# GpSimd makes all ten low halves of the held-back expert weights in the token stage

## The chip, the cores and the metric

The program runs on one core of one Trainium2 chip, in one launch. What is measured is the device time of that launch in microseconds (us). PE is the matrix engine (TensorE), DVE the vector engine, ACT the scalar engine, POOL is GpSimd, and SP is the engine that issues most of the DMAs.

## The reference

The computation is one transformer layer on 8 sequences of 256 tokens of width 512 (2048 tokens): cross-attention, then a mixture-of-experts feed-forward block with two routed experts per token and one shared expert.

```
x = x + attention(layernorm(x), ctx) @ Wfc.T + bfc      # 32 query heads, 8 key/value groups, head width 16
h = layernorm(x)
w = two_best(softmax(h @ gate_weight.T))                # 8 experts in 4 groups, best 2 groups, best 2 experts
g, u = h @ gate_w[n].T, h @ up_w[n].T                   # n = 0..7, inner width 352; the shared expert has 704
routed = sum_n w[n] * ((silu(g) * u) @ down_w[n].T)
x = x + routed + (silu(h @ sh_gate.T) * (h @ sh_up.T)) @ sh_down.T
```

## The kernel before

All matrix products of the feed-forward block are made in float16 with a correction: each float32 weight is scaled by a power of two and cut into a **high half** (the scaled value rounded to float16) and a **low half** (what the rounding left, again in float16). PE then runs three products for one: high by high, high by low, low by high.

The gate and up weights are ten matrices (eight experts and the shared one in two parts), each handled as two pieces of 128 partitions by 1408 columns, so there are 20 pieces (`CUTS`). Ten are cut during attention. The other ten (`2 * HELD`, those of experts 0 to 4) are held back, since attention's own buffers lie where they go, and are cut in the **token stage**, the stage this text is about.

The token stage goes over 16 tiles of 128 tokens. For each tile t, in program order on each engine:

- PE: transposes the normalised tile t-2 (line 1439), transposes the attention output of tile t+1 (line 1422), multiplies tile t by Wfc (line 1430, 8 matmuls), and makes the gate logits of tile t-3 (line 1448).
- ACT: copies the transposed tile t-2 out twice (lines 1065 and 1066), copies the transposed attention output of tile t+1 out (line 1060, `ot_evac`), makes a square root (line 1074), copies logits (line 1070), then makes the high half of piece h = t-2 (line 1100, `first_part`), then normalises tile t (line 1079). PE's line 1430 of a tile cannot start before ACT's line 1060 for that tile.
- DVE: residual sum (line 1931), statistics (lines 1933 to 1935), low half of the transposed tile t-2 (line 1917), the reciprocal square root (lines 1689 to 1697), and the shift of the normalisation (line 1940). After every odd tile up to 11 it makes the low half of one held-back piece (line 1965), for h = 1, 3, 5, 7, 9.
- GpSimd: makes the low halves for h = 0, 2, 4, 6, 8. [...]
- SP issues the loads and stores of the tiles.

The raw pieces come by DMA (704 KB each) into a **ring of three buffers**, `stage_p3`. GpSimd issues these loads (line 815, `load_held`). Three are issued at the stage's start. The load of piece h+3 goes into the buffer of piece h, so it is issued when the low half of h is done, whoever made it:

```
pool.wait_ge(gu_cut_v, h // 2 + 1)          # odd h, before: GpSimd waits for DVE's low half
if h + 3 < 2 * HELD:
    load_held(h + 3)
```

ACT's `first_part(h)` waits for the landing of piece h, and stands in ACT's in-order queue between the work of two tiles. GpSimd's scaling of piece h waits for `first_part(h)` (`gu_first`). After the ten pieces GpSimd cuts two shared down matrices in the same manner (lines 884 and 888), which PE first needs at line 1512, in the stage that follows.

Of the kernel before, what the change touches and what calls it, by code (L numbers as in the profile page):

```python
# [26 lines left out]
ALU = mybir.AluOpType  # L27
# [18 lines left out]
CUTS = 2 * (NE + SH)  # L46
# [27 lines left out]
HELD = 5  # L74
CUTS_P2 = CUTS - 2 * HELD
# [5 lines left out]
def build(nc, x, ctxT, wqT, wkvT, wfcT, bfc, gwT, wgu, wdn, out):  # L81
# [17 lines left out]
    with ExitStack() as ctx:  # L99
# [3 lines left out]
        def sem(name):  # L103
            return ctx.enter_context(nc.semaphore(name))
# [11 lines left out]
        def words(at, n):  # L116
            return weights[:, at:at + n]
# [22 lines left out]
        def cut_place(h):  # L140

            e = h // 2
            at = 2 * (GU0 + e * GU_W if e < NE else SHGU0 + (e - NE) * GU_W) + h % 2 * HALF
            return weights16[:, at:at + HALF], weights16[:, at + GU_W:at + GU_W + HALF]
# [43 lines left out]
        stage_p3 = [words(KV_0 + s * HALF, HALF) for s in range(2)] + [words(DN0 + DN_W, HALF)]  # L188
# [47 lines left out]
        w_scale, w_inv = w_scale_i[:].bitcast(F32), w_inv_i[:].bitcast(F32)  # L236
# [139 lines left out]
        half_max_done, w_max_done, w_max_t, w_max_b0, w_max_b, w_max_tt, scale_done = (  # L376
            sem("half_max_done"), sem("w_max_done"), sem("w_max_t"), sem("w_max_b0"), sem("w_max_b"), sem("w_max_tt"), sem("scale_done"))
        gu_ld = [sem(f"gu_ld{s}") for s in range(3)]
        gu_first, gu_scaled, gu_cut, gu_cut_v = sem("gu_first"), sem("gu_scaled"), sem("gu_cut"), sem("gu_cut_v")
        ln16_done, xt_first, x_cut_high = sem("ln16_done"), sem("xt_first"), sem("x_cut_high")  # L380

        soft_in, soft_exp, sel_done, pre_ready, slots_done, offs_done = (
# [42 lines left out]
        def _(sp):  # L425
# [50 lines left out]
            def load_down(e):  # L476

                if e < NE - 1:
                    sp.dma_start(dn_raw(e + 1), wdn[e]).then_inc(dn_ld_late if e in (5, 6) else dn_ld, 16)
                else:  # L480
                    for j, to in enumerate((zero_row, ln16_sb, dn_tail)):
                        sp.dma_start(to[:], wdn[e, :, j * D:(j + 1) * D]).then_inc(dn_ld_last, 16)
# [144 lines left out]
            def h_rows(w):  # L627
                s = w % 2
                sp.wait_ge(h_cut, w + 1)
                if w >= 2:  # L630
                    sp.wait_ge(dn_done, w - 1)
                sp.dma_start(hT[s][:].rearrange("p a j t -> p (a j) t"), h_sb[s][:].bitcast(F16),
                             transpose=True).then_inc(hT_ld[s], 16)
# [10 lines left out]
            def load_shared(t, s):  # L644
                sp.dma_start(xT[s], tile_of(xnT_dram, t)).then_inc(sx_ld[s], 16)

            def load_res_x2(t, s):
                sp.dma_start(tok_in[s], tile_of(x2_dram, t)).then_inc(x2_ld[s], 16)

            def store_base(t, s):  # L650
                sp.wait_ge(y_evac, 2 * t + 2)
                sp.dma_start(tile_of(x2_dram, t), tok_in[s]).then_inc(base_st[s], 16)
# [3 lines left out]
            for w in range(B0):  # L656
                t, c = w // 2, w % 2
                if c == 1 and 2 <= t < EARLY - 2:
                    sp.wait_ge(u_ready, w + 1)
                    load_shared(t + 2, t % 2)  # L660
                if w >= 4 and c == 0:
                    store_base(t - 2, t % 2)
                if w > 0:
                    h_rows(w)
                if w == 1:
                    for s in range(2):
                        load_res_x2(s, s)
                    sp.wait_ge(dn_cut, SH)
                if w == 2:
                    sp.wait_ge(gu_cut, CUTS - HELD)  # L670
                    sp.wait_ge(gu_cut_v, HELD)
                    sp.wait_ge(fc_ready, TILES)
                    sp.wait_ge(xb_done, TILES)
                if w == 6:
                    sp.wait_ge(u_ready, 4)
                if 1 <= w < 8:
                    load_down(w - 1)
                if w == 2 * (EARLY - 3) + 1:
                    sp.wait_ge(table_ready, 1)
                    load_down(NE - 1)  # L680
                if w >= 5 and c == 1 and t < EARLY:
                    sp.wait_ge(base_st[t % 2], 16 * ((t - 2) // 2 + 1))
                    load_res_x2(t, t % 2)
# [53 lines left out]
            for w in range(C0, TOTAL):  # L737
                m, c = (w - C0) // 2, (w - C0) % 2
# [31 lines left out]
        def _(pool):  # L770
# [43 lines left out]
            def load_held(h):  # L814
                nc.gpsimd.dma_start(stage_p3[h % 3], wgu[h // 2, :, h % 2 * HALF:(h % 2 + 1) * HALF]).then_inc(gu_ld[h % 3], 16)

            def scaled_weights(c):

                return stage_p2[c % 2] if c < CUTS_P2 else stage_p3[(c - CUTS_P2) % 3], w_scale[:, cut_order[c] // 2:cut_order[c] // 2 + 1]

            def scale_weights(c):
                stage, scale = scaled_weights(c)
                pool.wait_ge(gu_first, c + 1)
                nc.gpsimd.tensor_tensor(stage, stage, scale.broadcast_to([P, HALF]), ALU.mult).then_inc(gu_scaled, 1)  # L824

            def pool_cuts(c):

                return c + 1 if c < CUTS_P2 else CUTS_P2 + (c - CUTS_P2) // 2 + 1

            def second_part(c):  # L830
                stage, _ = scaled_weights(c)
                high, low = cut_place(cut_order[c])
                pool.wait_ge(gu_scaled, pool_cuts(c))
                nc.gpsimd.tensor_tensor(low, stage, high, ALU.subtract).then_inc(gu_cut, 1)  # L834
                pool.wait_ge(gu_cut, pool_cuts(c))
# [60 lines left out]
            for c in range(CUTS_P2, CUTS):  # L896

                h = c - CUTS_P2
                if h % 2 == 0:
                    scale_weights(c)  # L900
                    second_part(c)
                else:
                    pool.wait_ge(gu_cut_v, h // 2 + 1)
                if h + 3 < 2 * HELD:
                    load_held(h + 3)
            for c in range(SH):
# [24 lines left out]
            for q in range(2 * EARLY):  # L931
                t, m = q // 2 + q % 2 * EARLY, q // 2 - 2
# [272 lines left out]
        def _(pe):  # L1205
# [393 lines left out]
            def slot_up(m, s, n=None):  # L1599
                pe.wait_ge(xt_evac, m + 1)  # L1600
                if n is not None:
                    pe.wait_ge(sx_ld[s], n * 16 + (16 + SX_SEEN))
                gate_up(m + B0, s, xT[s], routed_gu(m))
# [4 lines left out]
            early_tile(EARLY - 1, 1, EARLY // 2 - 1, first=lambda: slot_transpose(0, 0, 0),  # L1608
                       second=lambda: slot_transpose(1, 1, 0))
            pe.wait_ge(offs_done, 1)  # L1610
            pe.wait_ge(gu_cut, CUTS - HELD)
            pe.wait_ge(gu_cut_v, HELD)
            slot_up(0, 0)
            early_down(EARLY - 1, 0)
            slot_transpose(2, 0, 1)
# [58 lines left out]
        def _(dve):  # L1674
# [245 lines left out]
            def residual_norm(t, s, n):  # L1920
                link = chain(t * LN2_STEPS + links)
                dve.wait_ge(fc_ready, t + 1)
                if isinstance(t, int) and t < 2:
                    dve.wait_ge(xb_done, TILES - 1 + t)
                else:
                    dve.wait_ge(r_ld[s], n * 16)
                dve.wait_ge(x2_stored[s], n * 16 + FREE)
                if not (isinstance(t, int) and t < 2):
                    dve.wait_ge(ln2_done, t - 1)
                residual = xb_sb[s] if isinstance(t, int) and t < 2 else res_in[s]  # L1930
                nc.vector.tensor_tensor(x2_sb[s], bank[2 + s][:], residual, ALU.add).then_inc(x2_done, 1)
                dve.wait_ge(x2_done, t + 1)
                link(nc.vector.bn_stats(stats[:, 0, :], x2_sb[s]))
                link(nc.vector.bn_aggr(mv[:, s, :], stats[:, 0, :]))
                nc.vector.tensor_scalar(var_e[:, 0:1], mv[:, s, 1:2], EPS, None, ALU.add).then_inc(var_done, 1)
                if not (isinstance(t, int) and t < 2):
                    cut_rows(t - 2, s)
                dve.wait_ge(std_done, t + (BLOCKS + 1))
                newton(link, 1, rstd[:, s:s + 1])
                nc.vector.tensor_scalar(ln2_shift[:, s:s + 1], mv[:, s, 0:1], rstd[:, s:s + 1], -1.0,  # L1940
                                        ALU.mult, ALU.mult).then_inc(ln2_factors, 1)
# [16 lines left out]
            link = chain(links + 2 * LN2_STEPS)  # L1958
            down_scales(link)
            links += link.count[0]  # L1960
            def second_part(h):

                dve.wait_ge(gu_first, CUTS_P2 + h + 1)
                high, low = cut_place(h)
                nc.vector.scalar_tensor_tensor(low, stage_p3[h % 3], w_scale[:, h // 2:h // 2 + 1], high,
                                               ALU.mult, ALU.subtract).then_inc(gu_cut_v, 1)

            for t in range(2, TILES):
                residual_norm(t, t % 2, t // 2)
                if t % 2 == 1 and t < 2 * HELD + 2:  # L1970
                    second_part(t - 2)
            cut_rows(TILES - 2, 0)


# [531 lines left out]
```

## Time and profile before

| | us |
|---|---|
| median of 3 runs | 771.72 |
| lowest, highest | 770.38, 778.64 |
| the profiled execution, its own time | 773.04 |
| its span, first to last instruction | 771.3 |
| token stage in it, first to last line-1430 matmul | 284.7 to 365.3 |

The span is what the views of the trace count from: a time such as 346.41 is 346.41 us after the first instruction. The profiled execution is 1.3 us above the median of the runs, and 1.7 us of its time lie outside the span. A row of a timeline gives the start, the time it took, the engine, the line, the operation, and in square brackets the idle time of the engine just before it with what ended that. The mean granted clock of TensorE was 0.995 of full.

### The profile page before, as it was taken

What the parts mean: (1) busy time and instruction counts of PE and PEld (TensorE: products, weight loads), DVE (VectorE), ACT (ScalarE), POOL (GpSimd) and SP (SyncE); (2) the same over time, 40 slices, a digit from 0 to 9 for tenths busy, and PEclk for the clock granted to TensorE, in tenths of its full rate; (3) what the DMA queues carried; (4) which work ended last, traced back from release to release, by engine and by line L of the source; (5) the groups of instructions that cost most, each with busy time, mean ns of one, the idle gap of its engine ahead of it and who ended that gap; (6) DMA issues with size and microseconds to landing.
All of it is one profiled execution on the core that took longest, in us unless ns stands there. A gap on an engine that the chain in (4) does not pass through costs nothing.

```text
span 771.3 us, 15970 instructions
## 1 busy us (share of the span) xinstructions
PE 748.0 (97%) x5151; PEld 404.5 (52%) x5152; DVE 567.5 (74%) x1194; ACT 424.4 (55%) x860; POOL 267.4 (35%) x222
## 2 busy tenths in 40 slices
PE   6998999999999999999999999999999999999997
PEld 4553533444444335666655656555555555555554
DVE  5777779999999977887689886555555555446767
ACT  3666568988888875776624543343434343323231
POOL 3263007999995303657000101111111111016331
PEclk9999989999999999999999999999999999999999
DMA  9898846575655799996678556777777779549995
GB/s 331 336 406 252 252 158 202 170 208 170 181 178 158 248 356 331 367 381 224 192 203 243 138 134 160 178 180 177 180 177 177 180 180 216 128 110 280 306 259 164
DMA packets 161336, 171.04 MB, mean 222 GB/s; under 512 B 103616, under 2 KB 117440, under 8 KB 160768
## 3 DMA queue, kind: packets, MB, share of 16 engines
q1 hardware_dynamic: 149724, 128.36, 57.0%
q0 software_dynamic: 10960, 40.90, 17.1%
q10 hardware_dynamic: 596, 1.07, 0.4%
q8 instruction: 31, 0.51, 0.3%
q14 instruction: 25, 0.20, 0.1%
HBM read 104.87 MB, written 42.21 MB: 191 GB/s over the span
## 4 chain that ended last, share of the span: by engine, by line
PE 77%; DVE 13%; DMA 5%; issue 2%; ACT 2%; SPq 1%; ACTq 0%; DVEq 0%
PE psum L1500 31%; PE psum L1512 17%; DVE sb_rows L1732 6%; PE psum L1430 5%; PE psum L1349 5%; PE psum L1239 4%; PE psum L1335 4%; PE psum L1263 3%; DMA sb_weights<-in_wdn 2%; PE psum L1215 2%; DMA sb_weights<-in_x 1%; PE psum L1366 1%; PE psum L1448 1%; PE psum L1220 1%; DMA x_dram<-sb_rows 1%
## 5 line engine op out<-in xcount | busy, mean ns | idle before, releaser
L1500 PE MATMUL psum<-sb_weights,sb_rows 128*128 (+1 forms) x1608 | 250.8, 313 | 0.0
L1500 PEld LDWEIGHTS psum<-sb_weights,sb_rows 128*128 128x128 f16 x1608 | 157.3, 98 | 91.1 <-DMA sb_rows<-xnT_dram 0.3
L1732 DVE TENSOR_REDUCE sb_rows<-psum 128x4 f32<-128x1024 f32 x128 | 149.9, 1215 | 5.4 <-PE psum L1263 5.4
L1054 ACT ACTIVATE sb_weights<-psum 128x512 f32<-128x512 f32 x256 | 139.2, 595 | 23.5 <-PE psum L1335 20.5
L1512 PE MATMUL psum<-sb_weights,sb_hT 128*128 (+1 forms) x630 | 147.2, 379 | 0.0
L918 POOL DMA_INDIRECT sb_rows<-xn_rows,sb_slot_tok x39 | 38.4, 985 | 217.7 <-DVE sb_rows L2325 147.8
L1512 PEld LDWEIGHTS psum<-sb_weights,sb_hT 128*128 128x128 f16 x630 | 61.6, 98 | 64.8
L1128 ACT ACTIVATE psum<-psum 128x352 f32<-128x352 f32 x71 | 31.8, 448 | 114.4 <-DVE psum L1986 104.0
L1335 PE MATMUL psum<-sb_weights 50*128 50x512 f16 x256 | 87.0, 390 | 2.3 <-ACT sb_weights L1054 1.4
L1349 PE MATMUL psum<-sb_weights 128*32 128x256 f32 x1024 | 83.1, 397 | 0.3
L1263 PE MATMUL psum<-sb_weights 48*128 48x256 f16 x512 | 71.8, 275 | 0.7 <-DVE sb_rows L1732 0.7
L1986 DVE SCALAR_TENSOR_TENSOR psum<-psum,sb_inv_now,sb_h 128x352 f32<-128x352 f32 x39 | 23.1, 593 | 49.0 <-issue 40.1
L938 POOL DMA_INDIRECT sb_weights<-slot_y,sb_p_i x32 | 31.1, 971 | 80.5 <-DMA slot_y<-sb_rows 41.3
L1999 DVE SCALAR_TENSOR_TENSOR sb_h<-psum,sb_h_scale_i,sb_h 128x352 f16<-128x352 f32 x71 | 41.4, 583 | 23.8 <-ACT sb_h L1133 20.7
L1430 PE MATMUL psum<-sb_weights 128*128 128x512 f32 x128 | 58.2, 597 | 0.1
L1335 PEld LDWEIGHTS psum<-sb_weights 50*128 50x128 f16 x256 | 23.5, 93 | 55.6 <-ACT sb_weights L1054 46.7
L1123 ACT ACTIVATE sb_h<-psum,sb_inv_now 128x352 f32<-128x352 f32 x39 | 21.6, 553 | 55.0 <-PE psum L1500 55.0
L1133 ACT ACTIVATE sb_h<-psum,sb_h_scale_i 128x352 f16<-128x352 f32 x71 | 39.3, 553 | 17.2 <-DVE sb_h_scale_i L1991 16.1
L1239 PE MATMUL psum<-sb_weights 128*128 128x512 f16 x192 | 44.9, 380 | 2.9 <-issue 1.6
L824 POOL TENSOR_TENSOR sb_weights<-sb_weights,sb_w_scale_i 128x1408 f32<-128x1408 f32 x15 | 38.0, 2531 | 23.0 <-ACT sb_weights L1100 22.2
L1123 ACT ACTIVATE sb_h<-psum,sb_w_inv_i 128x352 f32<-128x352 f32 x32 | 17.7, 554 | 50.2 <-PE psum L1500 42.8
L834 POOL TENSOR_TENSOR sb_weights<-sb_weights 128x1408 f16<-128x1408 f32 x15 | 42.9, 2863 | 1.2
(275 smaller groups left out, 1016.8 us busy)
## 6 DMA issues: line engine op xcount, KB each, us to landing
sb_weights<-in_wgu SPq DMA_DIRECT2D x20, 704.0 KB, 7.9
sb_weights<-in_wgu POOLq DMA_DIRECT2D x20, 704.0 KB, 6.0
sb_weights<-in_wdn SPq DMA_DIRECT2D x17, 768.0 KB, 6.4
slot_y<-sb_rows SPq DMA_DIRECT2D x39, 256.0 KB, 2.3
sb_weights<-q_parts SPq DMA_DIRECT2D x96, 64.0 KB, 2.8
x_dram<-sb_rows SPq DMA_DIRECT2D x24, 256.0 KB, 4.2
q_parts<-sb_weights SPq DMA_DIRECT2D x16, 256.0 KB, 4.0
sb_rows<-in_x POOLq DMA_DIRECT2D x16, 256.0 KB, 5.4
```

Of the source, the lines that this page charges most:

```text
L834: nc.gpsimd.tensor_tensor(low, stage, high, ALU.subtract).then_inc(gu_cut, 1)
L1054: nc.scalar.activation(probs[G % 2][:, kt, pair * 512:(pair + 1) * 512], bank[4 + f % 2], ACT.Exp, scale=exp_by[n]).then_inc(exp_done, 1)
L1123: nc.scalar.activation(silu_out[par], two_parts(bank[GU_BANKS[par][0]]), ACT.Silu, scale=inv).then_inc(sil_done, 1)
L1239: mm = nc.tensor.matmul(bank[Q_BANKS[n][m]], wq16[:, wp, k, m * P:(m + 1) * P], xnT[n % 2][:, xp, k, :], start=(k == 0 and i == 0), stop=( ...
L1263: mm = nc.tensor.matmul(bank[banks[qt] + side][:, h * SEQ:(h + 1) * SEQ], q_st[s][lo:hi, g, h, b * SEQ + qt * P:b * SEQ + (qt + 1) * P], k ...
L1335: nc.tensor.matmul(bank[4 + side].rearrange("p (h t) -> p h t", h=HH), k_st[s][lo:hi, g, b * SEQ + kt * P:b * SEQ + (kt + 1) * P], q_st[s] ...
L1349: mm = nc.tensor.matmul(bank[6][VW * c:VW * (c + 1), 0:SEQ], v_now, probs[G % 2][:, kt, c * SEQ:(c + 1) * SEQ], start=(kt == 0), stop=(kt ...
L1430: mm = nc.tensor.matmul(bank[2 + s][:], oT[s][:, k, :], wfc_sb[:, k, :], start=(k == 0), stop=(k == KD - 1))
L1500: mm = nc.tensor.matmul(bank[GU_BANKS[par][which]][:, 0:F], x_T[:, xp * D + k * P:xp * D + (k + 1) * P], gu(wp, k, which), start=(k == 0 a ...
L1512: mm = nc.tensor.matmul(bank[Y_BANKS[par]][:], hT[par][:, hp, j, :], dn(wp, j), start=(j == 0 and n == 0), stop=(j == NF - 1 and n == 2))
L1732: nc.vector.tensor_reduce(to[:, :, j // UB, :, j % UB, qt], psum[:, banks[qt] * 512:(banks[qt] + 2) * 512] .rearrange("p (a h k) -> p a h ...
L1999: nc.vector.scalar_tensor_tensor(h16[par][:, 1, 0:F], bank[GU_BANKS[par][1]][:, 0:F], h_scale[:, par:par + 1], h16[par][:, 0, 0:F], ALU.mu ...
```

## The change

GpSimd makes the low half of every held-back piece, with its two instructions, in the order of h. DVE makes none. The semaphore `gu_cut_v`, which counted DVE's low halves, is gone, and those who waited for it (GpSimd before a load, SP before a down load, PE before the first routed expert) wait for GpSimd's count `gu_cut` instead. The ring of three buffers, ACT's high halves and their places in its queue are as they were.

```diff
             for c in range(CUTS_P2, CUTS):
                 h = c - CUTS_P2
-                if h % 2 == 0:
-                    scale_weights(c)
-                    second_part(c)
-                else:
-                    pool.wait_ge(gu_cut_v, h // 2 + 1)
+                scale_weights(c)
+                second_part(c)
                 if h + 3 < 2 * HELD:
                     load_held(h + 3)
...
             for t in range(2, TILES):
                 residual_norm(t, t % 2, t // 2)
-                if t % 2 == 1 and t < 2 * HELD + 2:
-                    second_part(t - 2)
...
             pe.wait_ge(offs_done, 1)
-            pe.wait_ge(gu_cut, CUTS - HELD)
-            pe.wait_ge(gu_cut_v, HELD)
+            pe.wait_ge(gu_cut, CUTS)
```

On GpSimd, from the start of the token stage's pieces on, this stood in a row before. `sb_weights` is the large weight area, in which the ring lies too, and `in_wgu` the raw gate and up weights in memory.

```order
120 L824 TENSOR_TENSOR sb_weights<-sb_weights,sb_w_scale_i 128x1408 [waits gu_first]
121 L834 TENSOR_TENSOR sb_weights<-sb_weights 128x1408 [waits gu_scaled]
122 L815 DMA sb_weights<-in_wgu 128x1408 [waits gu_cut]
123 L815 DMA sb_weights<-in_wgu 128x1408 [waits gu_cut_v]
124 L824 TENSOR_TENSOR sb_weights<-sb_weights,sb_w_scale_i 128x1408 [waits gu_first]
125 L834 TENSOR_TENSOR sb_weights<-sb_weights 128x1408 [waits gu_scaled]
126 L815 DMA sb_weights<-in_wgu 128x1408 [waits gu_cut]
127 L815 DMA sb_weights<-in_wgu 128x1408 [waits gu_cut_v]
```

And this stands there in the changed kernel (its lines are one lower in number).

```order
120 L823 TENSOR_TENSOR sb_weights<-sb_weights,sb_w_scale_i 128x1408 [waits gu_first]
121 L833 TENSOR_TENSOR sb_weights<-sb_weights 128x1408 [waits gu_scaled]
122 L814 DMA sb_weights<-in_wgu 128x1408 [waits gu_cut]
123 L823 TENSOR_TENSOR sb_weights<-sb_weights,sb_w_scale_i 128x1408 [waits gu_first]
124 L833 TENSOR_TENSOR sb_weights<-sb_weights 128x1408 [waits gu_scaled]
125 L814 DMA sb_weights<-in_wgu 128x1408 [waits gu_cut]
126 L823 TENSOR_TENSOR sb_weights<-sb_weights,sb_w_scale_i 128x1408 [waits gu_first]
127 L833 TENSOR_TENSOR sb_weights<-sb_weights 128x1408 [waits gu_scaled]
```

Between two loads there now always stand two GpSimd instructions, where after every first load the next one followed at once. GpSimd has 20 of these instructions in the stage instead of 10.

On DVE, at the end of an odd tile, this stood before; `sb_ln_shift` is the last step of the tile and line 1931 the first step of the next.

```order
369 L1697 TENSOR_SCALAR sb_rstd<-sb_rs_a,sb_rs_b 128x1 [waits step]
370 L1940 TENSOR_SCALAR sb_ln_shift<-sb_mv,sb_rstd 128x1 [waits step]
371 L1965 SCALAR_TENSOR_TENSOR sb_weights<-sb_weights,sb_w_scale_i 128x1408 [waits gu_first]
372 L1931 TENSOR_TENSOR sb_rows<-psum,sb_rows 128x512 [waits x2_stored0,ln2_done,r_ld0,fc_ready]
373 L1933 BN_STATS sb_stats<-sb_rows 128x6 [waits x2_done]
```

And this stands there now.

```order
367 L1692 TENSOR_SCALAR sb_rstd<-sb_rs_a,sb_rs_b 128x1 [waits step]
368 L1935 TENSOR_SCALAR sb_ln_shift<-sb_mv,sb_rstd 128x1 [waits step]
369 L1926 TENSOR_TENSOR sb_rows<-psum,sb_rows 128x512 [waits x2_stored0,ln2_done,r_ld0,fc_ready]
370 L1928 BN_STATS sb_stats<-sb_rows 128x6 [waits x2_done]
```

DVE goes from one tile to the next with nothing between. The queues of ACT and PE hold the same instructions in the same order as before.

## Rows read from the trace of the kernel before

**Rows 1.** The page: busy time and share of the span of each engine.

```profile
PE 748.0 (97%) x5151; PEld 404.5 (52%) x5152; DVE 567.5 (74%) x1194; ACT 424.4 (55%) x860; POOL 267.4 (35%) x222
```

**Rows 2.** Busy times by stretch (us and count): ten tiles of the token stage, and after.

```profile
299.00:351.20 52.20, 52.15 (x242) 32.51 (x241) 45.45 (x106) 39.01 (x70) 30.90 (x17) 1.00 1.01 373
...
368.00:388.00 20.00, 19.86 (x132) 12.94 (x131) 12.28 (x39) 12.53 (x25) 0.00 (x0) 1.00 0.62 192
```

**Rows 3.** The chain that ended last, in order of time: start, us, what.

```profile
304.82 3.70 PE psum L1430 x8
...
365.35 0.70 DVE sb_rows L1931
```

**Rows 4.** Timeline of PE, tiles 11, 12 and 13.

```profile
341.24 3.60 PE L1430 MATMUL psum<-sb_weights 128*128 128x512 f32 x8
...
346.41 3.70 PE L1430 MATMUL psum<-sb_weights 128*128 128x512 f32 x8
...
350.75 0.64 PE L1439 MATMUL psum<-sb_ident,sb_rows 128*128 128x128 f32 x4
...
351.66 1.02 PE L1430 MATMUL psum<-sb_weights 128*128 128x512 f32 x2
```

**Rows 5.** Timeline of ACT, tiles 10 and 11 (pieces 8 and 9).

```profile
342.58 1.47 ACT L1100 ACTIVATE sb_weights<-sb_weights,sb_w_scale_i 128x1408 f16<-128x1408 f32 x1
...
345.76 0.60 ACT L1060 COPY sb_weights<-psum 128x512 f32<-128x512 f32 x1
...
346.89 1.47 ACT L1100 ACTIVATE sb_weights<-sb_weights,sb_w_scale_i 128x1408 f16<-128x1408 f32 x1
...
350.06 0.60 ACT L1060 COPY sb_weights<-psum 128x512 f32<-128x512 f32 x1
```

**Rows 6.** DVE's low halves: durations in ns, smallest, median, largest.

```profile
L1965 DVE SCALAR_TENSOR_TENSOR sb_weights<-sb_weights,sb_w_scale_i x5: 2581/2696/2761, 306.7 to 348.4; 128x1408 f16<-128x1408 f32 x5
```

**Rows 7.** Timeline of GpSimd, pieces 0 to 2.

```profile
302.44 2.53 POOL L824 TENSOR_TENSOR sb_weights<-sb_weights,sb_w_scale_i 128x1408 f32<-128x1408 f32 x1 [10.13 <-ACT sb_weights L1100]
305.05 2.86 POOL L834 TENSOR_TENSOR sb_weights<-sb_weights 128x1408 f16<-128x1408 f32 x1
308.20 0.58 POOL L815 DMA_DIRECT2D sb_weights<-in_wgu  x1 [0.30 <-POOL sb_weights L834]
309.69 0.55 POOL L815 DMA_DIRECT2D sb_weights<-in_wgu  x1 [0.91 <-DVE sb_weights L1965]
312.86 2.53 POOL L824 TENSOR_TENSOR sb_weights<-sb_weights,sb_w_scale_i 128x1408 f32<-128x1408 f32 x1 [2.63 <-ACT sb_weights L1100]
```

**Rows 8.** GpSimd's two instructions: ns, smallest, median, largest, all 15 of each.

```profile
L824 POOL TENSOR_TENSOR sb_weights<-sb_weights,sb_w_scale_i x15: 2523/2532/2534, 124.9 to 344.2; 128x1408 f32<-128x1408 f32 x15
...
L834 POOL TENSOR_TENSOR sb_weights<-sb_weights x15: 2857/2862/2874, 127.5 to 346.8; 128x1408 f16<-128x1408 f32 x15
```

**Rows 9.** Loads of held-back pieces, from issue to landing: the last one, then all ten.

```profile
L815 POOL DMA_DIRECT2D sb_weights<-in_wgu x1: 579/579/579, 339.5 to 339.5; - x1
DMA to landing us min/median/max: 5.8/5.8/5.8
...
DMA to landing us min/median/max: 5.8/6.9/9.5
```

**Rows 10.** The same for the ten like loads in attention (line 812).

```profile
DMA to landing us min/median/max: 4.4/4.8/8.6
```

**Rows 11.** The end of GpSimd's work, and PE's first use of a shared down matrix.

```profile
363.53 3.10 POOL L888 TENSOR_TENSOR sb_weights<-sb_weights 128x1536 f16<-128x1536 f32 x1
...
380.67 2.10 PE L1512 MATMUL psum<-sb_weights,sb_hT 128*128 128x512 f16 x9
```

**Rows 12.** Busy times by stretch, early attention; the eighth figure is TensorE's clock.

```profile
100.00:104.00 4.00, 2.92 (x22) 1.04 (x20) 3.50 (x5) 1.62 (x4) 0.00 (x0) 1.00 0.56 155
104.00:108.00 4.00, 3.54 (x20) 1.16 (x22) 2.60 (x5) 2.77 (x6) 0.00 (x0) 0.62 0.58 184
108.00:112.00 4.00, 4.00 (x31) 1.18 (x28) 1.75 (x4) 2.54 (x5) 0.00 (x0) 0.52 0.37 104
```

More of the change, by code:

```diff
@@ L378, in build @@
         gu_ld = [sem(f"gu_ld{s}") for s in range(3)]
-        gu_first, gu_scaled, gu_cut, gu_cut_v = sem("gu_first"), sem("gu_scaled"), sem("gu_cut"), sem("gu_cut_v")
+        gu_first, gu_scaled, gu_cut = sem("gu_first"), sem("gu_scaled"), sem("gu_cut")
         ln16_done, xt_first, x_cut_high = sem("ln16_done"), sem("xt_first"), sem("x_cut_high")
@@ L669, in _ @@
                 if w == 2:
-                    sp.wait_ge(gu_cut, CUTS - HELD)
-                    sp.wait_ge(gu_cut_v, HELD)
+                    sp.wait_ge(gu_cut, CUTS)
                     sp.wait_ge(fc_ready, TILES)
@@ L826, in pool_cuts @@
             def pool_cuts(c):
-                return c + 1 if c < CUTS_P2 else CUTS_P2 + (c - CUTS_P2) // 2 + 1
+                return c + 1
             def second_part(c):
@@ L1960, in _ @@
             links += link.count[0]
[L1961 to L1966, printed above, removed]
             for t in range(2, TILES):
                 residual_norm(t, t % 2, t // 2)
-                if t % 2 == 1 and t < 2 * HELD + 2:
-                    second_part(t - 2)
             cut_rows(TILES - 2, 0)
```

## The prediction

> **What bounds the kernel now.** I read the page first: PE is busy for 97% of the span, DVE for 74%, ACT for 55%, GpSimd for 35% [rows 1]. That is an average over stages, so I went to the stage that the change touches. By stretches, PE is busy for 52.15 of 52.20 us there, DVE for 45.45, ACT for 39.01 and GpSimd for 30.90 [rows 2]. The chain that ended last agrees: from 304.82 to 365.3 it is PE and nothing else [rows 3]. So the token stage is held by PE, and neither DVE nor GpSimd is on the path.
>
> PE's timeline gives the pace. The projections (line 1430) of tiles 11, 12 and 13 start at 341.24, 346.41 and 351.66 [rows 4], 5.17 and 5.25 us apart. The odd 0.08 is a wait: ACT's copy for tile 12 ran from 345.76 to 346.36, and PE began 0.05 us later. The high half before that copy started at 342.58 [rows 5]. This gives the link I use below: a projection starts 346.41 - 342.58 = 3.83 us after the start of the high half that precedes its copy in ACT's queue, if nothing holds it longer. For piece 9 the same link leaves room: its high half started at 346.89, which frees tile 13 at 350.72, and PE came there at 351.66. So ACT can be **0.94 us** late at piece 9 before PE notices.
>
> **The change, part by part.**
>
> *DVE's five low halves go.* They took 2.70 us each at the median, 5 x 2.70 = 13.5 us of DVE [rows 6]. DVE is not on the path, so what this gives is only the lateness that they pass to ACT: the 0.08 us at every second tile. Over the five odd pieces that is 5 x 0.08 = 0.4 us at most. It is not an extra term where ACT is late for another reason, as below.
>
> *GpSimd gets five more pairs.* A pair is 2.53 us, a step of 0.08, and 2.86 us: from 302.44 to 307.91, 5.47 us [rows 7]. The two durations hardly vary over 15 instances (2.523 to 2.534 and 2.857 to 2.874 us, [rows 8]), whether DVE was in a low half or not, so I expect neither a gain nor a loss in them. Then come 0.29 us until the load is issued and 0.58 us for the issue: 302.44 to 308.78, **6.35 us for one piece** with its load. Before, GpSimd did one piece in two tiles, 10.42 us. Now it would have to do one in 5.2 us, and can't. Its loads go out every 6.35 us from 308.21 on: the load of piece h+3 at 302.44 + 6.35 h + 5.77. For the last load, piece 9 (h = 6), this is 302.44 + 38.10 + 5.77 = 346.31. Before, it went out at 339.48 [rows 9], because DVE's low halves let two loads go out almost together, at 308.20 and 309.69 [rows 7].
>
> *The landing.* In the stage a load took 5.8 to 9.5 us from issue to landing [rows 9]. The 9.5 is the last of three issued at once. The last load of all, which went out alone, took 5.8 with the same tile traffic around it. In the changed kernel every load after the first three goes out alone, so I take **5.8**. The bounds are the smallest of like loads in attention, 4.4, beside less traffic [rows 10], and 9.5. Piece 9 then lands at 346.31 + 5.8 = 352.11. ACT came to its high half at 346.89 before [rows 5]; it would now stand there for some 5 us, with the copies that PE needs queued behind it.
>
> One rule of the Trainium skill bears on this term. The page DMA: Bandwidth & Descriptors, in the section on the anatomy of one DMA from GpSimd, gives about 2.0 us plus the bytes over 436 GB/s; for 704 KB that is an estimate of 3.65 us. No load in the rows is that short (4.4 is the least, [rows 10]), and by the page's figure piece 9 would land at 349.96 and the sum below would be +2.1 instead of +4.2.
>
> *What PE loses.* With the link of 3.83 us, tile 13's projection starts at 352.11 + 3.83 = 355.94 instead of 351.66: 4.28 us late. Pieces 5 to 8 are late as well, but that is no further term, since the lateness grows from piece to piece and the last contains it. Piece 5 is the first to be late: it is issued at 302.44 + 12.70 + 5.77 = 320.91 and lands at 326.7, while ACT would come there at about 326 (346.89 less four tiles of 5.21). From there each tile takes 6.35 us instead of 5.2, and (6.35 - 5.2) x 4 = 4.6, less the slack of 0.94 and plus the lateness of piece 5 of 0.7, is 4.4, which agrees. Tile 14 then starts 5.17 after tile 13 and not 5.25 as it did with ACT just late, so 0.08 comes back: **+4.2 us**.
>
> *What lies behind.* GpSimd needs no load for pieces 7 to 9, so its rhythm there is 5.47 + 0.3 = 5.77: the last low half ends at 302.44 + 7 x 6.35 + 2 x 5.77 + 5.47 = 363.9, and the two down matrices, about 5.87 us each, at 375.6, where they ended at 366.6. PE first needs them at 380.67 [rows 11], and then 4.2 later. That cover is 9 us, so this is nothing. SP's wait before a down load and PE's before the first routed expert ask for counts that are complete at 363.9, before PE's first down product; they are nothing too. Can the 4.2 us be given back later? In the 20 us after the stage PE is busy for 19.86 [rows 2], so there is no idle time to take it up: all of it reaches the end.
>
> **The sum.** The profiled execution would go from 773.04 to 777.2; the median of the runs lies 1.3 lower, and I set the forecast on it: 771.72 + 4.2 = **775.9 us**, 0.5% slower.
>
> **Rivals.**
>
> *Loads land faster than 5.8.* With 4.4 us piece 9 lands at 350.71 and the sum is +2.8: 774.5. For it: in the new rhythm a tile takes 6.35 us with 1.98 MB (five tiles' moves of 256 KB and one piece) instead of 5.2 us, 312 GB/s, where the stretch had 373 [rows 2], and no second load competes. Against it: the lone load with 5.8 already had that. Chance 0.18. The page's estimate of 3.65 belongs here and would give 773.8.
>
> *Loads land slower.* The bound of 9.5 gives 4.2 + 3.7 = +7.9: 779.6. This would need GpSimd's own computing, which now follows each issue at once, to delay the transfer. The ten loads in attention were each followed by other GpSimd work and had a median of 4.8, which speaks against it. Chance 0.08.
>
> *TensorE's clock falls.* PE would stand idle for about 1.2 us in each of tiles 9 to 13, before the transpose that needs ACT's normalised tile and again before the projection. In the trace the clock was granted at 1.0 until PE was busy for only 2.92 of 4 us, and then it averaged 0.62 and 0.52 over the next 8 us (the lower of its two levels is 1.2 GHz, half of full), while PE was busy for 7.54 of 8 [rows 12]. A stretch of 7 us at half clock holds 3.5 us of work back, giving 4.2 + 3.5 = +7.7: 779.4. Against it: PE would be busy for 5.15 us of each tile's 6.35, and its idle time comes in two pieces of some 0.6 us. Chance 0.08.
>
> *DVE's relief wins, and the time is not slower.* If ACT were never kept waiting for a piece, the stage would run at 5.17 us throughout and gain 0.4: 771.3. The mechanism is real, and the point from which it decides is the landing: tile 13 would come at about 351.3, so piece 9 would have to land by 347.5, 1.2 us after its issue. The least in the rows is 4.4. Chance 0.04.
>
> **Chances and range.** The forecast gets 0.62; the rivals 0.18, 0.08, 0.08 and 0.04. The range has to take in both fast and slow landing and the clock, and the runs of the kernel before differ by 1.3 us at their lower end (770.38 to 771.72). From 4.4 us of landing on the lower run, 773.2, with something for the page's estimate, to the two rivals at the top: 772.5 to 779.8. A measurement here can tell about 1%, 7.7 us, from no change. Only the slow-landing and clock rivals come to that, on its edge, and the highest run of before (778.64) shows that a median can be pushed: 0.12 for slower by over 1%, 0.01 for faster, 0.87 within 1%.
>
> **What the changed profile would show.** GpSimd's timeline should have pair, load, pair, load with no idle time but the 0.3 before a load, 6.35 us apart from 302.4. ACT's high halves should be released by the DMA of the piece from about piece 5 on, not by its place in the queue. PE's projections should be 5.2 apart up to about tile 8 and 6.35 apart from 9 or 10 to 13, and PE should show idle time of some 4 us in all, ended by ACT. DVE should be busy for 13.5 us less. The prediction is wrong if the pieces land before ACT comes to them, if GpSimd's pair is not 5.47 us, if the time lost in the stage is won back after it, or if the clock drops in it.

## The result, and the profile after

| | us |
|---|---|
| before, median of 4 runs (lowest, highest) | 771.92 (770.38, 778.64) |
| changed, median of 4 runs (lowest, highest) | 780.62 (777.14, 782.56) |
| ratio, 95% interval | **1.0089** [1.0051, 1.0127] |
| profiled execution before and after, span | 771.3 and 780.8 |

The kernel is slower by 0.9%, and the interval lies wholly above 1. Of 771.92 us that is 6.9 us, between 3.9 and 9.8. The quotient of the medians in the table would be 1.0113; the ratio, which goes by all the runs, and its interval are what the text uses. The profiled execution of the changed kernel, 782.56 us by its own time, is the slowest of its four.

The page of the changed kernel first, with the busy times and the head of the chain that ended last.

```profile
PE 750.2 (96%) x5151; PEld 404.5 (52%) x5152; DVE 555.1 (71%) x1189; ACT 424.6 (54%) x860; POOL 294.2 (38%) x232
...
PE 63%; DVE 15%; DMA 7%; POOL 5%; issue 4%; ACT 3%; SPq 2%; another core or an unknown queue 0%; ACTq 0%; DVEq 0%
```

Against [rows 1], DVE is busy for 12.4 us less (13.5 were forecast) and GpSimd for 26.8 us more, which is the change itself. PE does the same 5151 matmuls. GpSimd now has 5% of the chain.

Busy times of the token stage, some twelve tiles of it, answer to [rows 2]: us and count of PE, weight loads, DVE, ACT and GpSimd, then the granted clock, the DMA share and GB/s.

```profile
299.00:361.00 62.00, 58.57 (x260) 35.40 (x258) 36.05 (x110) 43.02 (x79) 54.87 (x26) 1.00 0.96 334
```

Before, PE was idle for 0.05 us in [rows 2]. Now it is idle for 3.43 us, while GpSimd is busy for 54.87 of 62.00. The clock stayed at 1.00 here.

GpSimd's timeline, the first piece, the start of the second and the last load, answers to [rows 7]. Line 823 is the scaling of a piece, line 833 the subtraction.

```profile
303.05 2.53 POOL L823 TENSOR_TENSOR sb_weights<-sb_weights,sb_w_scale_i 128x1408 f32<-128x1408 f32 x1 [9.96 <-ACT sb_weights L1096]
305.66 2.87 POOL L833 TENSOR_TENSOR sb_weights<-sb_weights 128x1408 f16<-128x1408 f32 x1
308.82 0.60 POOL L814 DMA_DIRECT2D sb_weights<-in_wgu  x1 [0.30 <-POOL sb_weights L833]
309.44 2.55 POOL L823 TENSOR_TENSOR sb_weights<-sb_weights,sb_w_scale_i 128x1408 f32<-128x1408 f32 x1
...
347.23 0.60 POOL L814 DMA_DIRECT2D sb_weights<-in_wgu  x1 [0.30 <-POOL sb_weights L833]
```

There is no idle time left but the 0.30 us before each load (and steps of under 0.1 us), and the seven loads go out from 308.82 to 347.23: (347.23 - 308.82) / 6 = 6.40 us apart. GpSimd's own pace sets when a buffer comes free. The chain that ended last says the same: from 303.05 to 347.23 it is GpSimd and nothing else, then the load of piece 9, then ACT and PE.

```profile
303.05 2.54 POOL sb_weights L823
...
347.23 6.48 DMA sb_weights<-in_wgu
...
355.11 0.80 ACT sb_rows L1075
...
357.40 3.70 PE psum L1426 x8
```

The seven loads from issue to landing, for comparison with [rows 9]:

```profile
L814 POOL DMA_DIRECT2D sb_weights<-in_wgu x7: 597/597/602, 308.8 to 347.2; - x7
...
DMA to landing us min/median/max: 5.9/7.1/7.9
```

The waits between 298 and 385, by line and what was waited for: us in total, times, longest.

```profile
ACT sb_weights L1096 <- DMA sb_weights<-in_wgu: 12.8, 7, 3.2
...
PEld psum L1426 <- ACT sb_weights L1056: 2.6, 5, 0.6
PEld psum L1435 <- ACT sb_rows L1075: 2.4, 4, 1.1
```

ACT's high halves (now line 1096) wait for the landing of their piece seven times, from piece 3 on (the forecast had said from about piece 5 on); before, this row didn't exist. PE in turn waits for the two ACT instructions queued behind the high half, the normalisation (line 1075) and the copy for the projection (line 1056). In the timeline of ACT and then of PE, around piece 9 and tile 13, this reads as follows.

```profile
353.73 1.47 ACT L1096 ACTIVATE sb_weights<-sb_weights,sb_w_scale_i 128x1408 f16<-128x1408 f32 x1 [3.19 <-DMA sb_weights<-in_wgu]
355.11 0.80 ACT L1075 ACTIVATE sb_rows<-sb_rows,sb_ln_shift,sb_rstd 128x512 f32<-128x512 f32 x1
...
356.76 0.59 ACT L1056 COPY sb_weights<-psum 128x512 f32<-128x512 f32 x1
```

```profile
305.44 3.70 PE L1426 MATMUL psum<-sb_weights 128*128 128x512 f32 x8
...
350.44 3.70 PE L1426 MATMUL psum<-sb_weights 128*128 128x512 f32 x8 [0.35 <-ACT sb_weights L1056]
...
355.96 0.66 PE L1435 MATMUL psum<-sb_ident,sb_rows 128*128 128x128 f32 x4 [1.03 <-ACT sb_rows L1075]
...
357.40 3.70 PE L1426 MATMUL psum<-sb_weights 128*128 128x512 f32 x8 [0.35 <-ACT sb_weights L1056]
```

The load of piece 9 is issued at 347.23 and lands at 353.73, 6.5 us later. ACT starts at that moment, PE's transpose follows at 355.96, the projection of tile 13 at 357.40. From tile 4 (305.44) to tile 13 it is 51.96 us, where it was 351.66 - 304.82 = 46.84 [rows 3, 4]: **5.1 us lost between two points, both inside the stage**. By starts, tiles 4 to 8 are still 5.2 us apart (326.22 is tile 8), and from tile 8 on 6.24, 6.37, 5.43, 6.18 and 6.96.

The span grew by 9.5 us, more than that. The rest is 0.6 us before tile 4, 0.7 at 461, and 3.2 near the end, where PE waited in the last expert's products.

```profile
719.12 2.12 PE L1508 MATMUL psum<-sb_weights,sb_hT 128*128 128x512 f16 x9 [2.12 <-DMA sb_hT<-sb_h]
...
725.41 2.12 PE L1508 MATMUL psum<-sb_weights,sb_hT 128*128 128x512 f16 x9 [0.60 <-DMA sb_hT<-sb_h]
```

These two waits are in none of three further traces of the same kernel (below), so nothing ties them to the change.

### The profile page after: what moved, and what is told of

Same layout as the page of the kernel before. It is cut to its first block, busy times and chain, and to the rows that moved or that the text cites. A ratio compares the mean times of both kernels' runs of the same rounds, so it can differ in the third digit from the quotient of the medians.

```text
span 780.8 us, 15974 instructions
## 1 busy us (share of the span) xinstructions
PE 750.2 (96%) x5151; PEld 404.5 (52%) x5152; DVE 555.1 (71%) x1189; ACT 424.6 (54%) x860; POOL 294.2 (38%) x232
## 4 chain that ended last, share of the span: by engine, by line
PE 63%; DVE 15%; DMA 7%; POOL 5%; issue 4%; ACT 3%; SPq 2%; another core or an unknown queue 0%; ACTq 0%; DVEq 0%
PE psum L1496 27%; PE psum L1508 14%; DVE sb_rows L1727 6%; PE psum L1345 4%; PE psum L1235 4%; PE psum L1331 3%; POOL sb_weights L833 3%; POOL sb_weights L823 2%; PE psum L1426 2%; PE psum L1259 2%; DMA sb_weights<-k_parts 2%; PE psum L1211 2%; DMA sb_weights<-in_x 1%; DMA sb_hT<-sb_h 1%; PE psum L1362 1%
## 5 line engine op out<-in xcount | busy, mean ns | idle before, releaser
L833 POOL TENSOR_TENSOR sb_weights<-sb_weights 128x1408 f16<-128x1408 f32 x20 | 57.3, 2863 | 1.6
L823 POOL TENSOR_TENSOR sb_weights<-sb_weights,sb_w_scale_i 128x1408 f32<-128x1408 f32 x20 | 50.8, 2539 | 11.0 <-ACT sb_weights L1096 10.0
```

## The experiments

Two theories stood against each other. **The ring**: GpSimd's lateness reaches PE only since the low half of piece h frees the buffer of piece h+3. **The amount of work**: GpSimd as such, with 20 instructions where it had ten, slows the stage, by whatever it shares with the others, and the price follows the count. Beside these stood the question whether DVE's relief is worth something. There were two sets of runs, each on one chip beside 23 runs of the kernel before. The four-buffer ring, DVE with piece 3, DVE with pieces 7 and 9 and the first repeat of the changed kernel stand beside a median of 772.38, the other four beside 773.51.

### A ring of four buffers

A fourth buffer is taken from space of the held-back weights that is written last (the place of piece 9's own result), and four loads go out at the start. Semaphores and buffers are taken in turn by four instead of three.

```diff
-         stage_p3 = [words(KV_0 + s * HALF, HALF) for s in range(2)] + [words(DN0 + DN_W, HALF)]
+         stage_p3 = [words(KV_0 + s * HALF, HALF) for s in range(2)] + [words(DN0 + DN_W, HALF), words(GU0 + (HELD - 1) * GU_W + GU_W // 2, HALF)]
-            for h in range(3):
+            for h in range(4):
                 load_held(h)
...
-                if h + 3 < 2 * HELD:
-                    load_held(h + 3)
+                if h + 4 < 2 * HELD:
+                    load_held(h + 4)
```

> The changed kernel with a fourth buffer in the ring: the load of piece h+4 goes out when the low half of h is done, and four loads go out at the start. GpSimd still makes all ten low halves, 6.4 us each. Theory (ring): PE was late only since the loads waited for GpSimd. Then piece 9 is issued after piece 5, at about 341 instead of 347.2, lands at about 347.5, ACT waits for at most 0.5 us, the projections stay 5.2 us apart, tile 13 starts 47.0 us after tile 4 (before 46.84, changed 51.96), and the time is within 1.5 us of the kernel before, some 5 us or more below the changed kernel. Rival (GpSimd is simply too much work for the stage): its rhythm is the same, so the stage stays 5 us longer. Rival (something outside the stage): the loss stays.

Measured: 773.88 us (12 runs), ratio 1.0017 [1.0000, 1.0035]. GpSimd has the same 20 instructions, and all but 1.3 us of the loss is gone. In the trace tile 13 comes 47.34 us after tile 4, where 47.0 was expected. What is left of the loss stands at the stage's start, in PE's timeline and in the waits of 302 to 320.

```profile
307.38 3.70 PE L1426 MATMUL psum<-sb_weights 128*128 128x512 f32 x8
...
313.39 3.70 PE L1426 MATMUL psum<-sb_weights 128*128 128x512 f32 x8 [0.35 <-ACT sb_weights L1056]
...
354.72 3.60 PE L1426 MATMUL psum<-sb_weights 128*128 128x512 f32 x8
```

```profile
DVE sb_rows L1926 <- DMA x_dram<-sb_rows: 4.1, 2, 2.6
DVE sb_rows L1926 <- DMA sb_rows<-xb_dram: 3.0, 1, 3.0
```

Tile 5 comes 6.01 us after tile 4 and not 5.2: DVE's residual sum waited for the tiles' own store and load, which ran beside four pieces issued together (the slowest of these loads took 11.5 us to land). So the fourth buffer cured one thing and brought another. From tile 5 to tile 13 (354.72) it is then 41.33 us, where it was 351.66 - 310.07 = 41.59 before: from tile 6 on the tiles come 5.15 us apart, without the 0.08 at every second one. That is DVE's relief, 0.26 us over eight tiles.

### Four buffers, the fourth load later

```diff
+            pool.wait_ge(gu_ld[1], 16 * CUTS_P2 // 2 + 16)
+            load_held(3)
```

Three loads go out at the start as before, and the fourth when the second has landed.

> The four-buffer ring with GpSimd making all ten, but the fourth load goes out when the second piece has landed and not with the first three. In the trace of the four-buffer kernel with four loads at once the stage lost 0.9 us between tiles 4 and 5, behind loads that landed late, and then ran 5.16 us a tile. Theory: spreading removes that, tile 13 starts 46.4 to 46.9 us after tile 4 (before 46.84), and the time is that of the kernel before within 1 us. Rival: GpSimd's steady work costs something else (the clock, DMA), and about +1.3 us stays.

Measured: 772.32 us (12 runs) beside 773.51, ratio 1.0004 [0.9987, 1.0021]. The stage of this kernel by its windows, and two pieces of GpSimd's timeline:

```profile
297.00:358.00 61.00, 61.00 (x278) 37.65 (x277) 38.43 (x121) 46.23 (x83) 55.40 (x27) 1.00 0.95 345
```

```profile
306.23 2.55 POOL L823 TENSOR_TENSOR sb_weights<-sb_weights,sb_w_scale_i 128x1408 f32<-128x1408 f32 x1
...
312.63 2.55 POOL L823 TENSOR_TENSOR sb_weights<-sb_weights,sb_w_scale_i 128x1408 f32<-128x1408 f32 x1
```

PE is busy for 61.00 of 61.00 us, though GpSimd is as busy (55.40) and as slow (6.40 us a piece) as in the changed kernel. That settles the main question: all ten low halves on GpSimd cost nothing that can be measured once the ring is one buffer deeper. DVE's relief brings nothing that can be measured either: with GpSimd's lateness out of the way, the kernel is where it was before, not ahead of it.

### Three buffers, GpSimd faster

GpSimd has one instruction for a held-back piece, the subtraction, and leaves the scaling out.

```diff
-                scale_weights(c)
-                second_part(c)
+                pool.wait_ge(gu_first, c + 1)
+                high, low = cut_place(cut_order[c])
+                nc.gpsimd.tensor_tensor(low, scaled_weights(c)[0], high, ALU.subtract).then_inc(gu_cut, 1)
+                pool.wait_ge(gu_cut, c + 1)
```

> The changed kernel with three buffers, but GpSimd leaves out the scaling of the held-back pieces and only subtracts, so a piece takes it 2.9 us and about 3.8 with its load; the low halves of experts 0 to 4 are then not the reference's. Ring theory: GpSimd is faster than the 5.2 us of a tile, no load is late, DVE is relieved too, and tile 13 starts 46.3 to 46.6 us after tile 4: time 0 to 1 us below the kernel before. That is also the whole worth of the relief of DVE. If the relief is worth more than 0.4 us it shows here.

Measured: 772.96 us (10 runs) beside 773.51, ratio 0.9995 [0.9976, 1.0015]. GpSimd's timeline:

```profile
304.56 2.85 POOL L900 TENSOR_TENSOR sb_weights<-sb_weights 128x1408 f16<-128x1408 f32 x1 [0.96 <-ACT sb_weights L1098]
307.71 0.58 POOL L814 DMA_DIRECT2D sb_weights<-in_wgu  x1 [0.30 <-POOL sb_weights L900]
309.55 2.85 POOL L900 TENSOR_TENSOR sb_weights<-sb_weights 128x1408 f16<-128x1408 f32 x1 [1.26 <-ACT sb_weights L1098]
```

Now GpSimd waits for ACT and not the other way round, the ring of three is enough, and the loss is gone. GpSimd also has half the work here, so this kernel alone would fit the amount of work too; the four-buffer kernel above decides between the two. It shows another thing: GpSimd stands idle for 1.0 to 2.4 us after each load that it issues, and yet the seven loads take 7.1 us at the median to land, as in the changed kernel. GpSimd's computing right behind the issue is not what made them longer than 5.8.

Tile 13 comes 46.83 us after tile 4, as before the change (46.84), where I had expected 46.3 to 46.6. That isn't because the relief of DVE is worth nothing. DVE's and then PE's timeline:

```profile
332.83 0.69 DVE L1928 TENSOR_TENSOR sb_rows<-psum,sb_rows 128x512 f32<-128x512 f32 x1 [2.60 <-DMA sb_rows<-xb_dram]
```

```profile
333.26 3.60 PE L1428 MATMUL psum<-sb_weights 128*128 128x512 f32 x8
...
338.66 3.70 PE L1428 MATMUL psum<-sb_weights 128*128 128x512 f32 x8
```

Up to tile 10 (333.26) the stage is 0.14 us ahead of the kernel before (31.02 us from tile 4, against 31.16). Then a load of the tokens' own rows lands late, DVE waits for it until 332.83, and tile 11 comes 5.40 us and tile 12 5.26 us after the tile before, which eats the gain. The spread four-buffer kernel has such waits too. These row loads took 6.7 us at the median here and 6.2 there, against 4.8 before; why isn't shown.

### DVE makes piece 3 alone

```diff
-                scale_weights(c)
-                second_part(c)
+                if h not in BY_DVE:          # BY_DVE = (3,)
+                    scale_weights(c)
+                    second_part(c)
+                elif h + 3 < 2 * HELD:
+                    pool.wait_ge(gu_cut_v, len([g for g in BY_DVE if g <= h]))
```

> The changed kernel with one low half given back to DVE, that of piece 3; GpSimd makes the other nine. Ring theory: from piece 3 on each load goes out some 5.8 us earlier, piece 9's at about 341.5, and the stage's loss is gone (tile 13 starts 47 to 47.5 us after tile 4). Time about 5 us below the changed kernel. Rival (amount of GpSimd work): one of five pieces back gives a fifth of the loss, 1 us.

Measured: 775.11 us (10 runs), ratio 1.0044 [1.0026, 1.0063]: half of the loss comes back. In the trace, though, tile 13 comes 50.43 us after tile 4, where I had expected 47 to 47.5. GpSimd's timeline around the piece, then DVE's one instruction:

```profile
313.64 2.86 POOL L835 TENSOR_TENSOR sb_weights<-sb_weights 128x1408 f16<-128x1408 f32 x1
316.80 0.60 POOL L816 DMA_DIRECT2D sb_weights<-in_wgu  x1 [0.30 <-POOL sb_weights L835]
318.29 0.53 POOL L816 DMA_DIRECT2D sb_weights<-in_wgu  x1 [0.89 <-DVE sb_weights L1966]
321.46 2.53 POOL L825 TENSOR_TENSOR sb_weights<-sb_weights,sb_w_scale_i 128x1408 f32<-128x1408 f32 x1 [2.65 <-ACT sb_weights L1101]
```

```profile
313.71 4.27 DVE L1966 SCALAR_TENSOR_TENSOR sb_weights<-sb_weights,sb_w_scale_i 128x1408 f16<-128x1408 f32 x1 [0.72 <-ACT sb_weights L1101]
```

DVE started 0.07 us after GpSimd's subtraction and took 4.27 us for what had taken 2.58 to 2.76 [rows 6]. It ended 1.48 us after the subtraction. That held DVE's statistics up, and through them ACT's normalisation and PE: tile 7's projection started at 316.17 and tile 8's at 323.73, 7.56 us apart, 2.4 lost. After it the ring lost another 1.2 us: piece 9 was issued 39.42 us after tile 4 started (at 340.03), 2.4 us earlier than in the changed kernel (41.79) where I had expected some 5.8, and ACT still stood 2.32 us for it until 347.37. My sum had left out what the mixed arrangement costs DVE. With 1.5 of 5.1 us back in the trace, this kernel lies nearer to the rival's 1 us than to the 5 of the ring, so by itself it doesn't tell the two apart; it is the 2.4 us at tile 8, a cost that neither had, that blurs it.

### DVE makes pieces 7 and 9

The same edit with `BY_DVE = (7, 9)`. GpSimd has four instructions fewer, but no load waits for these two pieces.

> The changed kernel with two low halves given back to DVE, those of pieces 7 and 9, whose buffers no load waits for. GpSimd does 11 us less and ends 11 us earlier. Ring theory: nothing changes for the loads, tile 13 still starts 51.5 to 52.5 us after tile 4, and the time is that of the changed kernel within 1.5 us. Rival (amount of GpSimd work, or its late end): two of five pieces back give at least 2 us, more than piece 3 alone gives.

Measured: 780.24 us (4 runs), ratio 1.0093 [1.0062, 1.0124], the changed kernel's own figure. Taking work off GpSimd where no load hangs on it gives nothing back. One disturbance goes with it, in GpSimd's and then DVE's timeline:

```profile
344.01 4.14 POOL L835 TENSOR_TENSOR sb_weights<-sb_weights 128x1408 f16<-128x1408 f32 x1
348.44 0.60 POOL L816 DMA_DIRECT2D sb_weights<-in_wgu  x1 [0.30 <-POOL sb_weights L835]
```

```profile
342.99 2.43 DVE L1966 SCALAR_TENSOR_TENSOR sb_weights<-sb_weights,sb_w_scale_i 128x1408 f16<-128x1408 f32 x1 [2.39 <-ACT sb_weights L1101]
```

Here DVE got in between GpSimd's scaling of piece 6, which ended at 343.92, and the subtraction, which took 4.14 us instead of 2.86. The load of piece 9 went out that much later, and tile 13 came 53.30 us after tile 4 instead of 51.96 (51.5 to 52.5 were expected). So this kernel pays 1.3 us of its own in the trace, and if the amount of work counted, at most that much is hidden under it.

### The changed kernel three times more

No edit, for what differs from one execution to the next.

> The changed kernel once more, for a second trace. In the first the stage cost 5.0 us, and further 0.7 us were lost at 461 and 3.2 us between 711 and 737, where PE waited for the transposing DMA of the hidden rows. If these belong to the change, they come again at the same places with the same size. If they are chance of the DMA queues, they come elsewhere or not at all, and the time is between 776.5 and 781.

Measured: 779.22 us (4 runs), ratio 1.0097 [1.0067, 1.0127].

> The changed kernel, a third trace. Its two traces lose 5.0 to 5.3 us in the stage, while its runs lie about 7 us above the kernel before, at a mean granted clock of 0.993 to 0.995 against 0.997. Theory: the waits of PE in the stage make the clock fall in some executions, and that is the rest; then a trace that has a stretch of half clock between 340 and 375 turns up. Rival: the rest is lost in the last stage by chance of the DMA queues, as the 3.9 us of the first trace.

> The changed kernel, a fourth trace, with the same question: whether a stretch of half clock lies in or right behind the stage, and whether the stage's own loss is again 5.0 to 5.3 us and the last stage's zero.

Measured: 779.45 and 779.20 us, one run each. From tile 4 to the first product of the next stage the four traces take 5.0, 5.3, 5.6 and 6.5 us more than before, 5.6 on average. In two of them TensorE's clock fell inside the stage. The windows of the third and then of the fourth trace:

```profile
340.00:350.00 10.00, 8.71 (x39) 5.24 (x37) 5.24 (x16) 5.63 (x9) 9.29 (x6) 1.00 0.94 309
350.00:355.00 5.00, 4.54 (x13) 3.01 (x14) 1.62 (x6) 3.40 (x8) 4.84 (x3) 0.66 0.89 327
```

```profile
340.00:350.00 10.00, 7.62 (x37) 4.80 (x36) 4.97 (x14) 5.39 (x10) 9.50 (x6) 1.00 0.93 310
350.00:355.00 5.00, 4.74 (x14) 2.38 (x15) 1.61 (x6) 4.47 (x10) 4.86 (x2) 0.66 0.74 260
```

PE was busy for 8.71 and 7.62 of 10 us, and then the clock averaged 0.66 over 5 us, which is 3.4 us at the lower of its two levels (1.2 GHz) and the rest at 2.4. The kernel in which DVE makes pieces 7 and 9 had such a stretch too, at 358. The three traces in which PE doesn't wait in the stage (before, four buffers with the spread load, one GpSimd step) had none there. Waits of PE alone don't bring it about: with piece 3 on DVE, PE was busy for 7.94 us of the 10 from 320 on, with one wait of 1.8 us, and the clock stayed at 1.00. Elsewhere such stretches come and go: the one that the kernel before had early in attention [rows 12] is found in three of the four traces of the changed kernel, and in the other one there is a shorter one in its place, at 65.

| kernel | tile 13 after tile 4, us | ratio to before |
|---|---|---|
| before | 46.84 | 1 |
| changed, four traces | 51.96, 52.22, 52.65, 53.52 | 1.0089, 1.0097 |
| DVE makes 7 and 9 | 53.30 | 1.0093 |
| DVE makes 3 | 50.43 | 1.0044 |
| four buffers | 47.34 | 1.0017 |
| four buffers, spread | 46.82 | 1.0004 |
| one GpSimd step | 46.83 | 0.9995 |

## Why the prediction was right, and where it was short

The forecast was 775.9 us, within 1% and slower. The ratio puts the changed kernel at 771.72 x 1.0089 = 778.6, in the range (772.5 to 779.8) and within 1%, near the edge of both; the median of its four runs, 780.62, lies just above.

**The bound and the path: right.** PE holds the stage, and DVE's and GpSimd's own busy times are not on the path. The lateness came in by the ring, as said, through ACT's queue. The three kernels that open the ring or speed GpSimd up show it, and the one that takes work off GpSimd behind the last load shows it from the other side.

**GpSimd's pace: right, 0.05 short.** Pair and load took 6.40 us against 6.35, because the scaling took 2.55 us instead of 2.53 and the issue 0.60 instead of 0.58. Over six pieces that is 0.3 us: the last load went out 347.23 - 303.05 = 44.18 us after GpSimd's first instruction, against 43.87 forecast.

**The landing: the term that was off.** I took 5.8 us, from the one load that went out alone. In the trace of the kernel before it was the shortest of the stage's seven later loads, whose median was 6.8; with that the sum would have been +5.2. Piece 9 took 6.5, and 6.7, 6.4 and 5.7 in the other three traces; the seven loads issued one by one had a median of 7.1 in the first trace, and since they went out 6.40 us apart, one was mostly still on its way when the next was issued. A single load was thus no measure of the term: the scatter of piece 9 alone is 1 us. The rival of faster landing, and with it the 3.65 us worked out from the Trainium skill's page DMA: Bandwidth & Descriptors, had nothing for it: no held-back load issued in the stage landed in under 5.7 us in the four traces. The rival of 9.5 us didn't come either.

**The link: 3.67 us against 3.83.** From landing (353.73) to tile 13's projection (357.40). With these three, 44.18 + 6.5 + 3.67 = 54.35 us from GpSimd's first instruction to tile 13, where it had been 351.66 - 302.44 = 49.22: 5.1 us, as the trace shows. The forecast was 4.3.

**DVE's relief: as small as forecast, and not seen in the times.** The forecast had 0.08 us of it in the sum and 0.4 as its bound. The mechanism was read rightly: with DVE free, the 0.08 at every second tile is gone, which gives 0.26 us over eight tiles in the four-buffer kernel and 0.14 over six in the one-step kernel. In the latter and in the spread one, waits for late row loads cost as much again, and no run's time could show a quarter of a microsecond.

**Nothing behind, nothing given back: right.** The last low half ended at 364.45 (363.9 forecast), and from tile 13 to the next stage's first product it is 15.8 us against 15.9 before.

**The clock: a rival with 0.08 that came in part.** It was priced at +3.5 us over 7 us of half clock. In two of four traces it came, for 3.4 us, behind a load of piece 8 that took 7.4 and 7.8 us. Tile 13 then came 5.81 and 6.65 us after tile 12 instead of 5.25, so there it cost 0.6 and 1.4 us. I had argued that PE's idle time comes in pieces of 0.6 us; in the fourth trace one wait was 2.4 us. Over all runs the mean granted clock of the changed kernel is 0.9937 (10 runs) and that of the kernel before 0.9970 (46 runs). Among the runs of before, one more hundredth of clock lost goes with 6.15 us, which would make this difference worth some 2 us; among the ten runs of the changed kernel it goes with only 1.9 us, which would make it 0.6. These are readings of averages, no experiment: nothing was run that holds the clock and leaves the waits.

**The sum.** Forecast +4.2, measured +6.9 (3.9 to 9.8). The waits alone account for 5.0 to 5.3, with the clock in the stage 5.6 on average. What is above that, 1.3 us, is within the interval. The traces leave little of it: the spans of the second to the fourth are 6.1, 6.4 and 6.1 us longer than that of before, and the stage with what lay ahead of its tile 4 makes up 6.0, 6.2 and 6.1 of that. Only the first had more behind the stage, 3.9 us of waits that didn't come again. The kernel before has only one trace here, and where the rest of the runs' difference lies, if there is any, isn't settled.

## What to carry to other kernels

Before work is moved to a slower engine, look at what its completion releases. Here the engine had time to spare by its busy share, yet its completion freed a buffer, the load stood behind it, and an in-order queue that the bounding engine needs stood behind the load; the price was about (the new pace less the tile's pace) times the pieces from where the slack ends, up to the last load, and not a matter of busy time. One more buffer took all of it away, as long as its load didn't go out with the others. Relief of an engine that is not on the path is worth at most the small waits that it passes on, here a quarter of a microsecond, and any late transfer can swallow that. And a term such as a landing should be taken from all like transfers of the stage, not from the one that looks most like the new case.

## What the runs showed of the hardware

DVE's low half (two inputs from SBUF) doesn't run beside GpSimd's scaling or subtraction. With GpSimd idle, DVE took 1.68 us for it, as piece 9 of the kernel in which DVE makes 7 and 9 shows:

```profile
356.54 1.68 DVE L1966 SCALAR_TENSOR_TENSOR sb_weights<-sb_weights,sb_w_scale_i 128x1408 f16<-128x1408 f32 x1 [4.12 <-ACT sb_weights L1101]
```

Started 0.07 us after the subtraction, it took 4.27 us and ended 1.48 us after it. Started while the scaling of piece 6 ran, it took 2.43 us and ended 1.50 us after the scaling; the subtraction behind it took 4.14 us instead of 2.86 and ended 2.73 us after DVE. In the kernel before, too, each of DVE's five ended 1.48 or 1.49 us after a subtraction, so its 2.70 us [rows 6] are a wait of 1.1 to 1.3 us and then its run. GpSimd's two durations didn't vary there [rows 8] since it was always DVE that waited. The Trainium skill states this on the page SBUF — State Buffer, in the section on SBUF's two separate sides: DVE and GpSimd share a port pair as an exclusive lock, and whichever starts first holds it for its whole instruction. These times agree with it. Who waits was decided by less than 0.1 us in two of these kernels, and with GpSimd as the late engine a lost race went into PE's time (2.4 us with piece 3, 1.3 us with pieces 7 and 9).
